# Context padded to 128 rows, its first quarter loaded in two halves, and six fillers fewer ahead of it

## What is computed

```python
x = x + xattn(_layernorm(x), ctx_1024, ctx_1024, Wq, bq, Wk, bk, Wv, bv, Wo, bo)
x = x + ffn(_layernorm(x), W_in, b_in, W_out, b_out)

# xattn: q, k, v are projections of 16 heads; k and v are padded with zeros to 2048 tokens
qf = jnp.fft.rfft(qt)
kf = jnp.fft.rfft(kt)
c = qf.real * kf.real + 1j * -(qf.imag * kf.imag)
corr = jnp.fft.irfft(c, n=Lq)
mean_value = jnp.mean(corr, axis=(1, 2))
weights, delay = jax.lax.top_k(mean_value, top_k)      # 15 delays
# softmax(weights) mixes v, taken at each delay; then the product with Wo

# ffn: x and hidden rounded to 16 bits, weights to 8 bits
hidden = gelu(x_sim @ W_in_sim + b_in)
out = quantize(hidden) @ W_out_sim + b_out
```

## Time and profile before

| | |
|---|---|
| median of 3 runs | 165.87 us (165.53 to 165.87) |
| the profiled execution | 165.92 us, of which the span is 163.8 us |
| TensorE busy | 154.5 us, 94% of the span |
| DVE, ACT, POOL busy | 126.1, 111.3, 40.4 us |
| read from HBM, written to it | 9.89 MB, 2.10 MB |

### The profile page before, as it was taken

One profiled execution on the slowest core, in us unless ns is written; L12 is line 12 of the kernel. 1 busy time (PEld: TensorE's weight loads), 2 busy tenths in 40 slices (PEclk: granted clock), 3 DMA queues, 4 the chain that ended last, 5 costly groups with the idle time before them and its releaser, 6 DMA issues.

```text
span 163.8 us, 2952 instructions
## 1 busy us (share of the span) xinstructions
PE 154.5 (94%) x1126; PEld 112.5 (69%) x1129; DVE 126.1 (77%) x269; ACT 111.3 (68%) x179; POOL 40.4 (25%) x43
## 2 busy tenths in 40 slices
PE   7999999999999999999999789999999789999990
PEld 5898476787666888996658564444445468888880
DVE  0007879999588759446999879999877799999963
ACT  3265512979862556464489979998889399999900
POOL 8002210008600073000059600199000033320000
PEclk9999999999999999999999999999999999999999
DMA  5999999400000000000000000000000000003306
GB/s 148 264 318 399 403 355 394 139 4 2 4 0 0 0 4 0 0 0 4 0 2 0 0 4 0 0 0 0 4 0 0 0 0 4 0 0 128 133 0 256
DMA packets 6284, 12.16 MB, mean 74 GB/s; under 512 B 576, under 2 KB 3904, under 8 KB 6016
## 3 DMA queue, kind: packets, MB, share of 16 engines
q1 hardware_dynamic: 6272, 11.99, 21.4%
HBM read 9.89 MB, written 2.10 MB: 73 GB/s over the span
## 4 chain that ended last, share of the span: by engine, by line
PE 84%; DVE 8%; ACT 5%; issue 1%; DVEq 0%; POOL 0%; POOLq 0%
PE ps L1256 15%; PE ps L1042 9%; PE ps L1021 9%; PE ps L1231 8%; PE ps L1226 8%; PE ps L999 5%; PE ps L1033 4%; PE ps L1164 4%; PE ps L986 4%; PE ps L1178 3%; PE ps L1074 2%; PE ps L1173 2%; DVE sm L849 2%; DVE sm L932 1%; PE ps L1085 1%; ACT arena L634 1%
## 5 line engine op out<-in xcount | busy, mean ns | idle before, releaser
L1256 PE MATMUL ps<-woutq,arena 128*128 128x256 f16 x256 | 28.7, 273 | 1.3 <-ACT arena L634 0.7
L1256 PEld LDWEIGHTS ps<-woutq,arena 128*128 128x128 f16 x256 | 24.7, 98 | 5.3 <-ACT arena L634 1.5
L619 ACT ACTIVATE arena<-ps,colv,sm 128x512 f32<-128x512 f32 x32 | 23.9, 777 | 2.3 <-PE ps L1231 0.5
L953 DVE SCALAR_TENSOR_TENSOR arena<-scr,sm,arena 128x1024 f16<-128x1024 int16 x16 | 21.3, 1372 | 0.0
L932 DVE TENSOR_REDUCE sm<-arena 128x1 f32<-128x1024 f32 (+1 forms) x17 | 18.9, 1148 | 2.5 <-ACT arena L619 2.5
L1231 PE MATMUL ps<-arena,winq 128*128 128x512 bf16 x64 | 18.6, 379 | 0.1
L1226 PE MATMUL ps<-arena,winq 128*128 128x512 bf16 x61 | 17.9, 379 | 0.3 <-DVE arena L897 0.3
L634 ACT ACTIVATE arena<-arena,sm 128x1024 f16<-128x1024 f32 x15 | 16.4, 1134 | 0.0
L1042 PE MATMUL ps<-wvo,arena 128*128 128x256 f32 x64 | 15.9, 389 | 0.0
L986 PE MATMUL ps<-ones 128*128 128x256 bf16 x96 | 14.1, 303 | 1.0 <-POOL ones L375 1.0
L1021 PE MATMUL ps<-arena,wqk 128*128 128x512 f32 x32 | 14.4, 598 | 0.0
(11 more groups left out here) (201 smaller groups left out, 283.1 us busy)
## 6 DMA issues: line engine op xcount, KB each, us to landing
arena<-x_dram SPq DMA_DIRECT2D x4, 512.0 KB, 9.5
out_dram<-arena SPq DMA_DIRECT2D x8, 256.0 KB, 2.1
arena<-ctx_in_dram SPq DMA_DIRECT2D x4, 448.0 KB, 6.0
tabs<-tab_dram SPq DMA_DIRECT2D x1, 1264.5 KB, 14.1
arena<-winT_dram SPq DMA_DIRECT2D x1, 1024.0 KB, 15.6
arena<-turn_dram SPq DMA_DIRECT2D x1, 1024.0 KB, 11.7
arena<-wout_dram SPq DMA_DIRECT2D x1, 1024.0 KB, 12.4
arena<-wqT_dram SPq DMA_DIRECT2D x1, 256.0 KB, 7.8
```

What stands on the lines that cost most here:

```text
L619: a.activation(H[:, f, 512 * c:512 * c + 512], bank("M1", n), ACT.Gelu, bias=colv[:, 6 + f:7 + f], scale=sc1[:, f:f + 1]).then_inc(S["h_re ...
L953: v.scalar_tensor_tensor(out=part, in0=scr16[:, n % 4, :], scalar=rf[:, f:f + 1], in1=piece(Hhi, n), op0=ALU.mult, op1=ALU.subtract).then_ ...
L1256: return t.matmul(o[k // 2][:, 256 * (k % 2):256 * (k % 2) + 256], part[:, t0:t0 + 128], woutq[:, f, :], start=start, stop=stop)
```

## The change

`AP`, the number of rows to which the context is padded, goes from 112 to 128. The first quarter of the context is loaded as two halves of two blocks each, with a semaphore each. TensorE takes the first half for both values of h (into the banks of CD0 and CD1), then the second half for both; quarters 2 to 4 are worked as before. The fillers ahead go from 20 to 14.

```diff
-AP = 112
+AP = 128
...
         ld_ctx = [sem(f"ld_ctx{i}") for i in range(4)]
+        ld_first = [sem(f"ld_first{i}") for i in range(2)]
...
             sp.dma_start(tabs[:, 0:n0], tab[:, 0:n0]).then_inc(S["ld_F"], 16)
-            for i in range(4):
+            for i in range(2):
+                sp.dma_start(cx[0:AP, 512 * i:512 * i + 512], ctx_in[0][:, 512 * i:512 * i + 512]).then_inc(ld_first[i], 16)
+            for i in range(1, 4):
                 sp.dma_start(cx[0:AP, 1024 * i:1024 * i + 1024], ctx_in[i]).then_inc(ld_ctx[i], 16)
...
-            keep_clock(0, 20)
+            keep_clock(0, 14)
             pe.wait_ge(S["ld_F"], 16)
-            for i in range(8):
+            def context(o, h, b):
+                return t.matmul(o[:, 128 * (b % 4):128 * (b % 4) + 128], cx[0:AP, 256 * b + 128 * h:256 * b + 128 * h + 128],
+                                F[0:AP, :], start=True, stop=True)
+
+            o = [take_bank(pe, "CD", h) for h in range(2)]
+            for part in range(2):
+                pe.wait_ge(ld_first[part], 16)
+                for h in range(2):
+                    for b in (2 * part, 2 * part + 1):
+                        last = context(o[h], h, b)
+                    if part == 1:
+                        done(last)
+            for i in range(2, 8):
                 bq, h = i // 2, i % 2
                 if h == 0:
                     pe.wait_ge(ld_ctx[bq], 16)
                 o = take_bank(pe, "CD", i)
-                for k in range(4):
-                    b = 4 * bq + k
-                    last = t.matmul(o[:, 128 * k:128 * k + 128], cx[0:AP, 256 * b + 128 * h:256 * b + 128 * h + 128],
-                                    F[0:AP, :], start=True, stop=True)
+                for b in range(4 * bq, 4 * bq + 4):
+                    last = context(o, h, b)
                 done(last)
```

## The result

The change makes the kernel slower: a median of 166.38 us (165.19 to 167.52, 20 executions) against 165.76 us (165.22 to 166.1, 20 executions) for the kernel before, a ratio of 1.0038 with a 95% interval of 1.0021 to 1.0055. The forecast was 165.2 us, 0.4% faster. Besides the median the spread has changed: 0.9 us before, 2.3 us after. The profiled execution took 167.19 us, of which the span is 165.2 us.

The account below looks back on a forecast made before the run. TensorE's queue was taken to bound the kernel up to 83 us. Six slots at 0.112 us gain 0.67, with the hand-over 0.73, taken as 0.70: 165.92 - 0.70 = 165.22, so 165.2 us, range 164.8 to 166.4.

Parts of the forecast that it names:

- The bound: Whole kernel up to 83 us: it is as long as TensorE's queue, so what leaves that queue moves all that follows.
- a gain reaches the end: Between the context and the end: other engines would not take up the 0.7 us, which should arrive whole.
- Part 1: Fillers ahead of the context: six fewer let TensorE start at 3.95 us, gaining 0.67 us, 0.70 with the hand-over.
- the prediction's own price: Clock's rise early in TensorE's queue: each us that it comes later costs 0.47 us.
- Part 2: First half's load: lands at 3.6 us, between 3.2 and 4.15, ahead of TensorE's 3.95 us, so no wait.
- The 3.75 us that stand beside the sum: First half's landing by the Trainium skill's figure: issue at 1.15, plus 2.0 fixed, plus 0.6 for its bytes.
- The upper bound: First half's latest landing, 4.15 us, at the first quarter's pace; it would leave a gain of 0.5 us.
- Part 3: Context loads on 128 rows: 393 GB/s, 1.33 us a quarter; quarters 2 to 4 land near 5.8, 7.1 and 8.4 us.
- rival B: Early loads slow from being early, not from 112 rows; quarters take 8/7 as long, 0.5 us slower, 166.4 us; chance 0.12.
- The need: When TensorE wants quarters 2 to 4: 7.0, 8.8 and 10.6 us, with all landing over 1 us early.
- Rival C: Clock rises later, through a pause at the hand-over or f32 passes; at 9.65 us, 0.7 us net loss, 166.6; chance 0.10.
- The part of C that blamed f32 passes: Context passes at the low clock: f32 passes bring the rise less soon than fillers; within the rival's chance of 0.10.

Follow-up runs that it names:

- contig14: Changed kernel (14 fillers) with the two halves read from an array of their own in HBM, rows of 2 KB back to back; median 166.79 us, ratio 1.0051.
- pad128: Kernel before with 128 rows instead of 112 alone, whole quarters and 20 fillers kept; median 165.71 us, ratio 0.9986.
- pad128b: Repeat of pad128: kernel before with 128 rows alone, whole quarters, 20 fillers; median 165.41 us, ratio 0.9985.
- fill20: Changed kernel with 20 fillers instead of 14, 128 rows and halves kept; median 166.34 us, ratio 1.0043.
- split112_20: Changed kernel with 112 rows and 20 fillers, so the two halves alone; median 166.75 us, ratio 1.0048.
- contig20: Changed kernel with 20 fillers and the two halves from an array of their own in HBM, rows back to back; median 166.68 us, ratio 1.0033.
- half_rest: Changed kernel with 20 fillers, first half loaded alone, then second half and second quarter as one 768 KB load; median 165.97 us, ratio 1.0014.
- again: The changed kernel itself measured once more, nothing altered; median 166.40 us, ratio 1.0048.
- fill17: Changed kernel with 17 fillers instead of 14; median 166.28 us, ratio 1.0037.
- fill24: Changed kernel with 24 fillers instead of 14; median 166.12 us, ratio 1.0028.
- split112: Changed kernel with 112 rows instead of 128, halves and 14 fillers kept; median 166.36 us, ratio 1.0031.
- contig14b: Repeat of contig14: changed kernel, 14 fillers, halves from an array of their own in HBM; median 167.03 us, ratio 1.0074.
- before14: Kernel before with 14 fillers instead of 20, 112 rows and whole quarters kept; median 166.77 us, ratio 1.0046.
- before14b: Repeat of before14: kernel before with 14 fillers instead of 20; median 167.09 us, ratio 1.0062.
- f32fill: Kernel before with its last 6 of 20 fillers replaced by 6 f32 passes; median 165.63 us, ratio 1.0004.

## Why the prediction was wrong

**The bound, and that a gain reaches the end: right.** TensorE's queue ahead of 83 us sets the time. L1007 to the end took 150.7 or 150.8 us in 20 profiles of 20, whether L1007 started at 12.24 or 15.04 us.

**Part 1, the price of fillers: right in size.** They start 0.213 us apart and end at 3.95 us. Where nothing else interfered (the profile of contig14), L1007 started 0.82 us sooner, against 0.70 forecast, and the execution took 165.17 us, against 165.2. Some luck is in it: the clock rose at 6.3 us instead of 6.7, worth 0.4 x 0.47 = 0.19 us by the prediction's own price. And it holds only while fillers are what sets the time, and in the changed kernel they are not: 14, 17, 20 and 24 of them give medians of 166.4, 166.3, 166.3 and 166.1 us.

**Part 2, the landing of the first half: wrong, and the first step that failed.** I took 3.6 us and bounds of 3.2 and 4.15. Measured were 4.56 and 4.48 us in the two profiles of the changed kernel, 4.71 to 5.83 with more fillers. TensorE stood still for 0.55 us in one and 0.47 in the other. I had priced a load by its bytes and took no account of its pattern: from an array with rows of 2 KB back to back the same 256 KB landed at 3.71, 3.79 and 3.82 us in three kernels, near the forecast, and at 4.32 when one of them was repeated. The 3.75 us that stand beside the sum rest on a figure that the Trainium skill, in the section named there, gives for loads issued by GpSimd; here SP issues them. The upper bound was taken from whole rows too and was therefore not a bound.

**Part 3, the pace of 128 rows: right for whole quarters, wrong with halves, and this is the step that costs the most.** pad128 shows the forecast of 1.33 us a quarter (pad128b 1.25 to 1.61), and the shape as the cause. So rival B is refuted as it was told: the early loads were slow through their 112 rows, not through being early. Both halves and rows were in one sum, though, and I wrote that splitting the quarter changes only the order in TensorE and one issue on SP. Its effect on the loads behind it was put at nothing, with margins of over 1 us as cover. The second quarter was to land at 5.8 us and landed at 7.87 and 7.39. Three pairs show it is the halves: fill20 against pad128 (same rows, same fillers, 166.34 against 165.71 and 165.41 us), split112_20 against the kernel before (166.75 against 165.76), contig20 against half_rest (166.68 against 165.97). In eight kernels with two halves at the head, with ten profiles between them counting the repeats, the second quarter landed between 7.4 and 8.5 us in nine and at 6.58 in one; with whole quarters or a single half, behind 20 fillers or 14 and 6 passes, at 6.1 to 6.8 in seven of seven. The median fits it: of the changed kernel's 32 executions 24 have L1007 between 12.9 and 14.1 us, which is where a second quarter landing at 7.4 to 8.5 us puts it, 5.5 us later. That this was so in the executions without a profile is an estimate from their spans.

**The need was wrong too.** I had TensorE ask for the second quarter at 7.0 us, from a clock that rises at 6.7 in every execution. The 20 profiles have the rise at 3.8 to 6.8 us in 18 cases. With the early ones TensorE is through the first quarter sooner and meets the late load sooner, and the load alone sets the time. Seven profiles have L1007 5.50 or 5.51 us behind the landing of the second quarter (again, fill17, fill24, split112, contig20, contig14b, before14): 48 passes of 0.112 us and the hand-over. The three runs that lay within 0.34 us, from which I read that the moment repeats, were too few. The Trainium skill, TensorE: Matmul & The Clock Gate, Part 1, says that it is not tied to a kernel's start, and the traces agree: 3.8 to 6.8 us in those 18, with the first filler always at 0.97 or 0.98.

**Rival C, the clock: it exists, and is the tail, not the median.** In the profile of the changed kernel and in that of fill20 the rise came at 10.0 and 9.9 us. I had worked out 9.65 and a total of 166.6; the execution took 167.19. The late load has no part in the difference, for TensorE did not wait for it; the context's start at 4.70 instead of 3.95 us costs 3.5 low passes, 0.39 us at full speed, and the rise at 10.0 instead of 9.65 another 0.16, together 167.15. The six executions of the changed kernel with L1007 at 14.4 us or later, the profiled one among them, are where such a clock puts it; the other five have no profile. In both profiles TensorE had paused for half a microsecond at the low level ahead of the context (0.55 and 0.54 us). A rise after 6.8 us was seen in no profile without such a pause, but three profiles with a pause of 0.31 to 0.47 us at the low level rose in time, at 5.0 to 6.6 us (again, contig14b, before14b), and before14, with the longest pause, was at the upper level from 3.9 us on. That a pause between 14 fillers and the context costs is shown by before14 and before14b (+1.0 and +1.3 us) against f32fill (-0.1). By which way, clock or loads, is not settled: profiles exist of one execution each, and the two of before14 show a late load and none a late clock. The part of C that blamed f32 passes is refuted by f32fill.

**In sum.** Of the two conditions that I named for the forecast, no pause and no late quarter, both were broken by the same thing, the two halves: the first landed late (by nine profiles, through its source pattern), and the pair of them put off the quarter behind. The step that failed is thus the price of the two half loads, too low for the first and put at nothing for what follows. The account is shown as far as "halves against whole"; what in the DMA queue does it is not. (A slip that changes nothing: the chances of a gain over 0.33 us add up to 0.705, not 0.68.) Rival B gave 166.4 us, and 166.38 was measured, but for a reason of its own: the mechanism, being early, is wrong.

## What to carry to other kernels

A load that is cut in two so that its first part comes sooner is not a change to that load alone; read what lands behind it. Test one at a time what is joined only by purpose: here the padding by itself came out about 0.15% faster and the halves lost 0.5%. And take the margin of a wait against the earliest time at which the waiting engine can ask, which here hangs on a clock that differs from execution to execution, and not against the one profile at hand.

## What the runs showed of the hardware

- Loads of whole quarters onto 128 rows run at 354 to 362 GB/s over 2.2 to 9.1 us and onto 112 rows at 266 to 285, at the same busy share of the DMA engines (0.99 to 1.01). So 64 KB more of zeros in each quarter made the fourth land sooner (9.08 and 9.51 us in pad128's two profiles against 10.59 and 9.79 in before and f32fill), while the first landed later (5.20 and 5.30 against 5.05 and 4.88).
- Two loads of half a quarter in a row (256 KB, or 224 with 112 rows) put off the whole quarter behind them by 1 to 2 us in nine profiles of ten; with one of them (one profile), or one load of 512 KB in 2 KB pieces (two profiles), the quarter behind was complete at 6.1 to 6.8 us.
- A first load of 256 KB that reads 2 KB out of every 4 KB of HBM took 3.3 to 4.7 us from issue to landing (five profiles); from rows back to back it took 2.6 to 3.2 us (four profiles).
- The clock row of the page shows full grant from the start of the span, and the windows above show 1.00 over 2.2 to 9.1 us, while products took 421 ns until 9.9 us. At the start of a kernel the durations of equal instructions tell the level (421 against 273 or 275 ns), the row does not.
- With TensorE at work from 0.98 us on, the upper level came between 3.8 and 6.8 us in 18 profiles; in the two with a pause of 0.54 and 0.55 us at the low level it came at 9.9 and 10.0 us.
